# One attention kernel, three engines rearranged: GpSimd takes a subtraction, and the head sums stream two tiles in place of three

## The reference

```python
xt = gn(x) as (b, n, c)
w = xt @ qkv_w.T                          # (b, heads, n, d)
s = sum(w_normed**2 over d)               # w normalised over the positions n
Pi = softmax(s * temp over the heads)     # (b, heads, n)
dots = sum(Pi / sum(Pi) * w**2 over n)    # (b, heads, d)
out = -(w * Pi) / (1 + dots)
y = x + out @ out_w.T + out_b
```

## Time and profile before

| what | value |
|---|---|
| device time, median of 3 runs | 867.71 us (867.59 to 868.12) |
| span of the profiled execution, first to last instruction | 864.9 us |
| what lies around it (median less span) | 2.8 us |
| busy PE, DVE, ACT, POOL | 851.6, 750.2, 528.3, 232.6 us |
| granted TensorE clock | 1.000 of full speed |
| images, of them in the loop | 32, 28 |

### The profile page before, as it was taken

How to read it: one execution, slowest core, us unless ns; L and a number is a source line. 1 busy time by engine, 2 the same in 40 slices (tenths; PEclk the granted TensorE clock), 3 DMA queues, 4 the chain that set the end, 5 groups by cost and what they waited for, 6 DMA issues and landing times.

```text
span 864.9 us, 14022 instructions
## 1 busy us (share of the span) xinstructions
PE 851.6 (98%) x4290; PEld 677.7 (78%) x4290; DVE 750.2 (87%) x1396; ACT 528.3 (61%) x680; POOL 232.6 (27%) x106
## 2 busy tenths in 40 slices
PE   7999999999999999999999999999999999999997
PEld 6767788777787777787777787777887777887776
DVE  7989889898888888888888898888898888898777
ACT  3567656567555677556676556676565675566642
POOL 2432123332123331133331233321233321233300
PEclk9999999999999999999999999999999999999999
DMA  7324665544664544664535654445655446645225
GB/s 279 119 79 153 225 229 185 185 148 169 225 227 161 197 146 181 226 223 160 180 150 198 228 213 168 163 145 220 227 186 196 141 163 225 228 175 186 88 86 197
DMA packets 45259, 157.42 MB, mean 182 GB/s; under 512 B 19866, under 2 KB 23962, under 8 KB 37274
## 3 DMA queue, kind: packets, MB, share of 16 engines
q1 hardware_dynamic: 36856, 154.10, 48.5%
q10 hardware_dynamic: 8354, 2.85, 1.3%
HBM read 104.47 MB, written 52.45 MB: 181 GB/s over the span
## 4 chain that ended last, share of the span: by engine, by line
PE 92%; DVE 4%; issue 1%; DMA 1%; ACT 1%; DVEq 0%; ACTq 0%
PE acc L678 86%; PE spread_ps L800 5%; DVE stats L906 1%; DVE WS L1041 1%; DMA PIB<-pi 0%; DMA X<-in_x 0%; DVE WV L1101 0%; DVE X L1149 0%; PE acc L655 0%; DVE WS L1080 0%; ACT WS L501 0%; DMA pi<-PIT 0%; DVE X L1116 0%; ACT WV L512 0%; PE spread_ps L815 0%
## 5 line engine op out<-in xcount | busy, mean ns | idle before, releaser
L424 POOL TENSOR_TENSOR XL<-XN,XH 128x1024 fp32r<-128x1024 f32 x93 | 222.9, 2414 | 571.7 <-ACT XH L529 548.2
L501 ACT ACTIVATE WS<-acc 128x1024 f32<-128x1024 f32 x96 | 98.4, 1026 | 240.5 <-PE acc L678 197.1
L678 PE MATMUL acc<-XH,W1H 128*128 128x512 f32 x574 | 177.3, 390 | 0.1
L678 PE MATMUL acc<-XH,W1L 128*128 128x512 f32 x574 | 176.8, 389 | 0.0
L678 PE MATMUL acc<-UH,W2H 128*128 128x512 f32 x558 | 172.6, 390 | 1.3 <-ACT WV L512 1.2
L678 PE MATMUL acc<-UH,W2L 128*128 128x512 f32 x558 | 172.3, 390 | 0.0
L678 PE MATMUL acc<-XL,W1H 128*128 128x512 f32 x576 | 146.2, 389 | 0.0
L678 PE MATMUL acc<-UL,W2H 128*128 128x512 f32 x558 | 145.3, 396 | 0.0
L1149 DVE SCALAR_TENSOR_TENSOR X<-acc,bias,X 128x1024 f32<-128x1024 f32 x93 | 116.3, 1276 | 31.0 <-PE acc L678 31.0
L678 PEld LDWEIGHTS acc<-UL,W2H 128*128 128x128 f32 x558 | 102.3, 188 | 32.2 <-issue 11.9
L678 PEld LDWEIGHTS acc<-XL,W1H 128*128 128x128 f32 x576 | 108.0, 188 | 22.7 <-POOL XL L434 0.3
(11 more groups left out here) (119 smaller groups left out, 501.3 us busy)
## 6 DMA issues: line engine op xcount, KB each, us to landing
PIB<-pi SPq DMA_DIRECT2D x94, 528.0 KB, 5.1
X<-in_x SPq DMA_DIRECT2D x31, 1536.0 KB, 6.3
out_y<-X SPq DMA_DIRECT2D x30, 1536.0 KB, 6.5
gathered<-stats_rows ACTq DMA_DIRECT2D x28, 72.0 KB, 5.1
pi<-PIT SPq DMA_DIRECT2D x94, 16.5 KB
X<-in_x SPq DMA_DIRECT2D x3, 512.0 KB, 4.7
out_y<-X SPq DMA_DIRECT2D x1, 1024.0 KB, 6.0
out_y<-X SPq DMA_DIRECT2D x2, 512.0 KB, 2.6
```

The costliest lines, as they stand in the source:

```text
L424: pool.tensor_tensor(XL[:, t, :], XN[:, t, :], XH[:, t, :].bitcast(F32), ALU.subtract).then_inc(xl_done, 1)
L501: act.activation(square_tile(i, t), acc[:, t, :], ACT.Square, accum_out=sumsq[:, t:t + 1]).then_inc(squared, 1)
L678: last = pe.matmul(out[:, h * BANK:(h + 1) * BANK], w[:, k, m * P:(m + 1) * P], r[:, k, h * BANK:(h + 1) * BANK], start=(n == 0 and k == 0 ...
```

## The change

For images 2 to 31 the squares of tiles 0 and 1 become one stream of the head sums. The columns of the first weights are laid out so that in tiles 0 and 1 partition p belongs to the same head (8 heads by 16 channels in each; tile 2 keeps 4 heads by 32). Then ACT scales the squares of tile 0 by 1/sumsq into a new tile `paired` (`scale_first`, between UH of tile 2 and the square of tile 2), DVE adds the squares of tile 1, scaled (`add_second`), and PE streams `paired` and tile 2: two tiles. The inverse sums of tiles 0 and 1 are made earlier on DVE (`pair_weights`), and `head_sum_weights` has only tile 2 left. Tiles 0 and 1 share one band of Pi rows: two PIB reads in place of three, of which the first waits for two pi writes; the total of attention becomes two instructions. UL of images 1 to 30 moves from DVE to POOL, ahead of XL in POOL's step. PE's order in the second product becomes: high terms of tile 0, head sums, high terms of tile 1, low terms of tiles 0 and 1, then tile 2. Not shown below: the layout of the setup (W1's columns, the head masks, the copy of out_w on POOL, now two copies), sizes and semaphores, and the uses of the bands in the first and last images.

```diff
@@ -44,10 +44,14 @@
-HEADSUM_STEPS = 3
+HEADSUM_STEPS = 5
+PAIR_STEPS = 2
+PAIRED = 2
+BAND = (0, 0, 1)
+BANDS = 2
-ATTENDED = 3 + 4
+ATTENDED = 3 + 5
...
@@ -259,9 +268,13 @@
-        def rows_moved(j, t, more=0):
-            return j.counts(16, more - (16 if t == 0 and True else 0))
+        def band_rows(t):
+            return PIB[:, BAND[t], :, 0:QUAD]
+        def paired_sums(j):
+            return j.follows(PAIRED)
...
@@ -369,15 +382,15 @@
                     sp.wait_ge(sm_step, j.counts(SM_STEPS, SM_STEPS))
-                    tiles = range(1 if by_pe(j) else 0, T)
-                    for t in tiles:
+                    for t in range(T):
                         rows = pi_dram[t * HPT:(t + 1) * HPT].rearrange("h (b q n) -> q (h b) n", b=BLOCKS, q=QUADS)
                         sp.dma_start(rows, PIT[:, t, :]).then_inc(pi_written[t], 16)
-                    for t in tiles:
-                        sp.wait_ge(pi_written[t], rows_moved(j, t, 16))
-                        heads = pi_dram[t * HPT:(t + 1) * HPT].unsqueeze(0)\
-                            .to_broadcast([D, HPT, BLOCKS * QUADS * (QUAD + 1)])
-                        sp.dma_start(PIB[:, t].rearrange("p b n -> p (b n)"), heads).then_inc(pi_spread[t], 16)
+                    for band, of_band in enumerate(BAND_HEADS):
+                        for t in range(of_band.start // HPT, of_band.stop // HPT):
+                            sp.wait_ge(pi_written[t], j.counts(16, 16))
+                        heads = pi_dram[of_band.start:of_band.stop].unsqueeze(0)\
+                            .to_broadcast([P // len(of_band), len(of_band), BLOCKS * QUADS * (QUAD + 1)])
+                        sp.dma_start(PIB[:, band].rearrange("p b n -> p (b n)"), heads).then_inc(pi_spread[band], 16)
...
@@ -424,7 +441,18 @@
+            def u_lo(j, t):
+                pool.wait_ge(uh_done, j.counts(T, t + 1))
+                wait_weighed(pool, j, t)
+                pool.wait_ge(m2_done, j.counts(T))
+                pool.tensor_tensor(UL[:, t, :], w_tile(j, t), UH[:, t, :].bitcast(F32),
+                                   ALU.subtract).then_inc(ul_done[t], 1)
             def step(i):
+                if i.follows(2) and has(i):
+                    for t in range(T):
+                        u_lo(i - 1, t)
                 for t in range(T):
...
@@ -539,9 +567,17 @@
+            def scale_first(i):
+                if has(i):
+                    act.wait_ge(headsum_step, i.counts(HEADSUM_STEPS, 2))
+                    act.wait_ge(squared, i.counts(T, 1))
+                    act.wait_ge(scores_done, i.counts(1))
+                    act.activation(paired[:], square_tile(i, 0), ACT.Copy, scale=inv[:, 1, 0:1]).then_inc(pair_step, 1)
...
@@ -550,6 +586,7 @@
                 u_hi(i - 1, 2)
+                scale_first(i)
                 square_w(i, 2)
...
@@ -705,6 +744,24 @@
                     product(acc[:, t, :], t, (W1H, W1L), (XH, XL), before, {}).then_inc(m1_done, 1)
+            def second_high(j, t):
+                pe.wait_ge(squared, (j + 1).counts(T, t + 1))
+                pe.wait_ge(w_kept, (j + 1).counts(T, t + 1))
+                for k in range(T):
+                    if t == 0:
+                        pe.wait_ge(uh_done, j.counts(T, k + 1))
+                    for n in (0, 1):
+                        term(acc[:, t, :], t, (W2H, W2L), (UH, UL), n, k)
+            def second_low(j, t):
+                for k in range(T):
+                    if t == 0:
+                        pe.wait_ge(ul_done[k], j.counts(1, 1))
+                    last = term(acc[:, t, :], t, (W2H, W2L), (UH, UL), 2, k)
+                last.then_inc(m2_done, 1)
...
@@ -794,11 +851,16 @@
                     pe.wait_ge(sm_step, i.counts(SM_STEPS))
-                for t in range(T):
+                if paired_sums(i):
+                    pe.wait_ge(pair_step, i.counts(PAIR_STEPS, PAIR_STEPS - PAIR_STEPS * PAIRED))
+                    streams = [(head_temp[:, 0, :], paired[:]), (headsum[:, T - 1, :], square_tile(i, T - 1))]
+                else:
+                    streams = [(headsum[:, t, :], square_tile(i, t)) for t in range(T)]
+                for n, (weights, squares) in enumerate(streams):
                     for q in range(QUADS):
-                        block_q = square_tile(i, t).rearrange("p (b q r) -> p q b r", q=QUADS, r=QUAD)[:, q]
-                        last = pe.matmul(scores[q * QUAD:(q + 1) * QUAD, 0:N // QUADS], headsum[:, t, :],
-                                         block_q, start=(t == 0), stop=(t == T - 1))
+                        block_q = squares.rearrange("p (b q r) -> p q b r", q=QUADS, r=QUAD)[:, q]
+                        last = pe.matmul(scores[q * QUAD:(q + 1) * QUAD, 0:N // QUADS], weights, block_q,
+                                         start=(n == 0), stop=(n == len(streams) - 1))
                 last.then_inc(scores_done, 1)
...
@@ -824,10 +886,18 @@
                 first_product(i, 2)
-                second_product(i - 1, 0, {(1, 2) if late else (2, 0): lambda: head_sums(i)})
-                second_product(i - 1, 1, {(1, 2): lambda: spread_heads(i), (2, 1): lambda: spread_totals(i)} if late else {})
-                second_product(i - 1, 2, {})
+                if late:
+                    second_product(i - 1, 0, {(1, 2): lambda: head_sums(i)})
+                    second_product(i - 1, 1, {(1, 2): lambda: spread_heads(i), (2, 1): lambda: spread_totals(i)})
+                    second_product(i - 1, 2, {})
+                    return
+                second_high(i - 1, 0)
+                head_sums(i)
+                second_high(i - 1, 1)
+                second_low(i - 1, 0)
+                second_low(i - 1, 1)
+                second_high(i - 1, 2)
+                second_low(i - 1, 2)
...
@@ -985,16 +1055,37 @@
                     return
-                link = chain(headsum_step, j.counts(HEADSUM_STEPS))
+                tiles = slice(T - 1, T) if paired_sums(j) else slice(0, T)
+                done = HEADSUM_STEPS - 3 if paired_sums(j) else 0
+                link = chain(headsum_step, j.counts(HEADSUM_STEPS, done))
                 dve.wait_ge(squared, j.counts(T, T))
-                link(dve.tensor_scalar(inv[:, 0, :], sumsq[:], NORM_FLOOR ** 2, None, ALU.max))
-                link(dve.reciprocal(inv[:, 1, :], inv[:, 0, :]))
+                link(dve.tensor_scalar(inv[:, 0, tiles], sumsq[:, tiles], NORM_FLOOR ** 2, None, ALU.max))
+                link(dve.reciprocal(inv[:, 1, tiles], inv[:, 0, tiles]))
                 if j.follows(1):
                     dve.wait_ge(temp_kept, 3)
-                link(dve.tensor_tensor(headsum[:], head_temp[:],
-                                       inv[:, 1, :].unsqueeze(2).to_broadcast([P, T, QUAD]), ALU.mult), follows=False)
+                weights = headsum[:, tiles, :]
+                dve.tensor_tensor(weights, head_temp[:, tiles, :], inv[:, 1, tiles].unsqueeze(2).to_broadcast(weights.shape),
+                                  ALU.mult).then_inc(headsum_step, HEADSUM_STEPS - 2 - done)
+            def pair_weights(j):
+                if not has(j):
+                    return
+                link = chain(headsum_step, j.counts(HEADSUM_STEPS))
+                dve.wait_ge(squared, j.counts(T, 2))
+                dve.wait_ge(scores_done, j.counts(1))
+                link(dve.tensor_scalar(inv[:, 0, 0:2], sumsq[:, 0:2], NORM_FLOOR ** 2, None, ALU.max))
+                link(dve.reciprocal(inv[:, 1, 0:2], inv[:, 0, 0:2]), follows=False)
+            def add_second(j):
+                if not has(j):
+                    return
+                dve.wait_ge(pair_step, j.counts(PAIR_STEPS, 1 - PAIR_STEPS * PAIRED))
+                dve.scalar_tensor_tensor(paired[:], square_tile(j, 1), inv[:, 1, 1:2], paired[:], ALU.mult, ALU.add)\
+                    .then_inc(pair_step, 1)
...
@@ -1027,18 +1118,17 @@
-                        if j.follows(2) or rows_moved(j, t) > 0:
-                            dve.wait_ge(pi_written[t], rows_moved(j, t))
+                        dve.wait_ge(pi_written[t], j.counts(16))
-                    dve.wait_ge(pi_spread[t], rows_moved(j, t, 16))
+                    dve.wait_ge(pi_spread[BAND[t]], j.counts(16, 16))
-                    dve.tensor_tensor_reduce(in_blocks(square_tile(j, t)), PIB[:, t, :, 0:QUAD],
+                    dve.tensor_tensor_reduce(in_blocks(square_tile(j, t)), band_rows(t),
...
@@ -1048,9 +1138,11 @@
-                    dve.wait_ge(u_step, j.counts(U_STEPS, T + k))
+                    dve.wait_ge(u_step, j.counts(U_STEPS, T + 1 + k))
-                    done = dve.tensor_reduce(total, PIB[:, :, :, QUAD], AX_X, ALU.add)
+                    dve.tensor_reduce(total[:, 0:2], PIB[:, 0, :, QUAD].unsqueeze(1).to_broadcast([P, 2, BLOCKS * QUADS]),
+                                      AX_X, ALU.add).then_inc(u_step, 1)
+                    done = dve.tensor_reduce(total[:, 2:3], PIB[:, 1, :, QUAD], AX_X, ALU.add)
...
```

(55 more changed lines are left out.)

17 lines of the change are left out of this document (9 added, 8 removed).

## The result

The changed kernel takes 982.47 us (median of 4 runs, 980.29 to 983.55) against 867.65 for the kernel before on the same chip (867.37 to 868.12): a ratio of 1.132, 95% interval 1.130 to 1.134. It is 115 us slower. The forecast was 962 us, slower, by a new wait of PE; the time lies 20 us above it and 7 us above the upper bound of 975.

What follows compares the result with a forecast made beforehand. PE, busy 98% of the span, was taken as the bound; a new wait of 3.5 us less 0.44 gain a step, taken as 95 us, gave 864.9 + 95 + 2.8 = about 962 us, range 950 to 975 (8-in-10: 855 to 975).

Steps and rivals of the forecast that it cites:

- PE's gain: Head sums on PE: two tiles streamed in place of three save 0.44 us a step, 13.2 us over 30 images.
- ACT's scaling: ACT's scaling of tile 0 before tile 2's square takes 1.1 us, hidden by idle time but for some 0.05 us.
- The order in which DVE and POOL hold each other: The add waits for POOL's second UL, the last tile's weights' product for the third; ULs take 2.3 to 3.7 us.
- the 2.90 us row: Start-up: an XL on POOL beside DVE's XN took 2.90 us instead of 2.41, read as POOL waiting for DVE.
- the two-input rule: DVE instructions with two SBUF inputs and POOL instructions reading SBUF exclude each other; whoever starts second waits until the other finishes.
- The new wait: PE's head sums wait for DVE's last weights, held behind POOL's ULs: 3.5 us a step, 3.06 net.
- The step that failed: Forecast sum: head sums start at 446.3 instead of 442.80; 3.5 less 0.44 is 3.06 a step, 92 us over 30.
- Rival 1: DVE and POOL don't hold each other up, or only POOL waits: faster, 854 to 863 us; chance 0.30.
- Rival 2: Only DVE's add waits for POOL, not the 32-column product: 1.06 us net a step, 900 us; chance 0.14.
- Rival 3: Pi's band 0 lands late (456.3), delaying dots, scaling and add; gain used up: 866 to 885 us; chance 0.10.

Runs made afterwards that it cites:

- experiment 10: Loop over images written out, no branches: experiment 9's kernel 857.46 us (from 885.54), experiment 7's 858.08 (from 861.95), all three ULs on POOL behind the weights 891.78 (from 914.07).
- experiment 5: Changed kernel with the pair's two-column DVE instruction (lower bound on the squares' sums) split into two of one column: 985.75 us, ratio 1.136 to the kernel before.
- Experiment 3: Changed kernel with 12 more matmuls on PE, product unused, ahead of the head sums' wait (the filled kernel): 960.83 us, ratio 1.1085 to the kernel before.
- experiment 4: Kernel before, UL on DVE, with six unused statistics instructions on DVE ahead of the head sum weights: 1004.51 us, ratio 1.158.
- experiment 6: Changed kernel with the product for tile 2's head sum weights (32 columns) made by ACT in place of DVE: 912.04 us, ratio 1.051 to the kernel before.
- experiment 7: Changed kernel with tile 0's UL on DVE ahead of the add, the other two on POOL behind the head sum weights: 861.95 us, ratio 0.9942 to the kernel before.
- experiment 2: Kernel before with only UL moved to POOL ahead of XL, nothing paired: 923.57 us, ratio 1.065.
- experiment 9: Kernel of experiment 7 with PE's high terms of tile 2 ahead of all low terms: 885.54 us, ratio 1.021 to the kernel before.

## Why the prediction was right in kind and wrong in size

**PE's gain: nearly right.** Forecast 0.44 a step, bounds 0.43 and 0.51. With no wait in the way (experiment 10) a step is 25.75 for 26.15: 0.40, a little under the lower bound. The head sums themselves save the 0.44 (1.00 us from their start to the next term, for 1.44); the terms behind them take 0.04 more. The head sums' records fell from 768 to 528, as said. The kernel without turns gains 10.6 us (868.01 to 857.46); 29 x 0.40 = 11.6, less the 0.8 that the first of the 30 steps loses, are 10.8.

**ACT's scaling: right.** 1.15 us in the trace of after, 1.1 forecast.

**The order in which DVE and POOL hold each other: right.** The add waits for the second UL, the product of 32 columns for the third, in the order of the forecast; UL takes 2.36 to 3.49 us, 3.32 in the median, forecast 2.3 to 2.5 unheld and up to 3.7 held. The Trainium skill, page "SBUF — State Buffer", section "Who interferes with whom", on which the forecast weighed its choice, agrees with the trace now in the direction that no row of before showed: the add 1.99 us beside UL and 1.28 without, the product 1.95 and 0.19. Not foreseen was that the pair's two-column instruction, with one tensor operand, is held too (2.17 us), although the one collision on record before, in the earlier trace rows, was with the same operation, TENSOR_SCALAR. That instruction reads one tensor, so the 2.90 us row was no case of the two-input rule that the prediction took it to agree with. The pair's instruction cost nothing that the add didn't cost again (experiment 5).

**The new wait: right for a PE at full clock.** Forecast 3.5 us from the old start of the head sums to the new, a net 3.06 a step, 962 us in all. Experiment 3, where the clock holds, has steps of 29.16 in the mean, against 26.20 in the kernel before: a net 2.96, and 960.83 us.

**The step that failed** is the sum of the forecast: "PE starts 0.06 later at 446.3 instead of 442.80: 3.5 us of new wait, less 0.44, is 3.06 a step, 92 us over 30 steps". It took PE to go on behind the wait as fast as before. Behind 2.8 us of idling the granted clock is 0.68 to 0.69 for 5.4 us, and head sums and high terms take 1.26 us longer than before although there is a tile less to stream. The mechanism was right and the sum lacked this term: 115 us measured, 92 to 103 forecast. Filling the wait gives back 21.6 us, about the 20 by which the forecast was short. Idling without POOL does the same (experiment 4), which shows that the idle time and not the collision lowers the clock. Part of the slower work is hidden: the wait is 2.77 in place of 3.54 where the clock holds, so that the net is at most 0.89 a step in the traces, and 0.72 by the medians (21.6 / 30).

A second, smaller term was missing too. In four turns of the loop DVE idles 3.9 to 4.2 us behind the branch, ahead of the final add. These four steps are 31.1 to 31.3 where the commonest are 30.0, so by the trace some 5 us of the 115 are the turns'. This is an estimate, as the changed kernel wasn't run with its loop written out. As the filled kernel has no such steps, about as much of its 21.6 us isn't the clock's.

**The rivals.** Rival 1 (no shutting out, or of POOL alone) fell with the add's 1.99 and the product's 1.95. Its time was 854 to 863: 857.5 and 861.9 are what the pairing gives once the collision is moved away. Rival 2 priced the add alone at 900; experiment 6 made that case and took 912. Rival 3's late band is real and small: in experiment 7 the first dot waits for PIB 27 times, 14.6 us in total, 0.5 each, and PE doesn't feel it.

## What to carry to other kernels

Before work goes to POOL, list what DVE does in the same stretch with two operands from SBUF, the small instructions ahead of a critical hand-over above all: 32 columns were held as long here as a whole tile, 70 us over the run with the lower clock that came of it. Put POOL's share where DVE reads PSUM or one operand: two of the three ULs, started after the last weights, with the third back on DVE, turned a loss of 13% into a gain of 0.6%, and of 1.2% with the loop written out. All three on POOL behind the weights pushed XL into the next dots and stayed a loss, 2.7% even with the loop written out. And a wait of PE is priced with the work behind it: here 2.8 us of idling cost up to another 0.9 us net in a step.

## What the runs showed of the hardware that was not expected

DVE's TENSOR_SCALAR on two columns (128x2), with a single tensor operand, took 2.17 to 2.41 us beside a running UL in all 30 steps of the changed kernel; the same on one column took 0.14 to 0.15 (experiment 5), and a RECIPROCAL on two columns 0.17.

PE's granted clock stayed at full behind idle times of 1.8 us in each step (experiment 2, mean 0.998), and fell behind 2.8 (the changed kernel, 0.68 to 0.69 in the stretch behind it) and 3.2 (experiment 4). In the changed kernel it didn't fall every time: four of the 30 steps stayed at full clock behind waits as long.

Behind the branch that turns the loop, DVE's next work came 5.6 to 6.0 us after it in experiment 9, in six turns, and without branches the same kernel is 28 us faster. The Trainium skill, page "Runtime: NRT & Kernel Launch", section "Instruction fetch mechanics", says that a taken branch breaks the sequential prefetch of instructions and can stall the engine until the target is fetched. The runs agree in that the stall goes with the branch; that it is the fetch itself, no row shows. In the stall shown, one packet moves on the instruction queue (378.9 to 384.6), but the kernel before moves two within 5.6 us behind its branch at 162.4 and has no stall there. In experiment 7 the turns cost only 3.9 us in all; what makes the difference stays open.
